# Sums of squares from ScalarE's accumulator in place of VectorE's reduction, in a fused decoder block

## The reference

```python
def rmsnorm(x, w, eps=1e-5):
    out = x * jax.lax.rsqrt(jnp.mean(x * x, axis=-1, keepdims=True) + eps)
    return out * w
q = rmsnorm((x @ Wq).reshape(B, T, H, D), q_rms_w)
k = rmsnorm((x @ Wk).reshape(B, T, H, D), k_rms_w)
scores = jnp.einsum('bthd,bshd->bhts', q, k) / sqrt(D) + bias   # causal
attn = softmax(scores)
y = rmsnorm(jnp.einsum('bhts,bshd->bhtd', attn, v), subln_w)
attn_out = y.transpose(0, 2, 1, 3).reshape(B, T, H * D) @ Wproj
```

## Time and profile before

| | |
|---|---|
| time, median of 3 runs | 435.72 us (434.96 to 436.02) |
| span of the profiled execution, first to last instruction | 432.9 us |
| TensorE busy | 401.9 us, 93% |
| its weight loads | 361.1 us, 83% |
| VectorE busy | 327.7 us, 76% |
| ScalarE busy | 254.4 us, 59% |
| GpSimd busy | 220.2 us, 51% |
| mean granted TensorE clock | 0.979 of full speed |
| chain that ended last, by engine | TensorE 86%, VectorE 5%, ScalarE 4% |

### The profile page before, as it was taken

One profiled execution on the slowest core, in us unless ns is written; L12 is line 12 of the kernel. 1 busy time (PEld: TensorE's weight loads), 2 busy tenths in 40 slices (PEclk: granted clock), 3 DMA queues, 4 the chain that ended last, 5 costly groups with the idle time before them and its releaser, 6 DMA issues.

```text
span 432.9 us, 9595 instructions
## 1 busy us (share of the span) xinstructions
PE 401.9 (93%) x2605; PEld 361.1 (83%) x2612; DVE 327.7 (76%) x1000; ACT 254.4 (59%) x750; POOL 220.2 (51%) x368
## 2 busy tenths in 40 slices
PE   4979999999999999999999999999999899999552
PEld 3668899999999999999999999999988677777321
DVE  0777987887797798788779779878822788888862
ACT  3486777677676776767767677676722333333321
POOL 3633667676675776767767677675501122222210
PEclk9999999999999999999999999999999999999965
DMA  8980010110101101011010110000000000000000
GB/s 223 316 251 2 2 36 3 38 37 0 36 0 36 36 0 36 0 36 36 0 36 0 36 36 0 0 0 0 0 2 0 2 0 15 12 14 12 13 14 24
DMA packets 21747, 14.52 MB, mean 34 GB/s; under 512 B 1760, under 2 KB 21472, under 8 KB 21728
## 3 DMA queue, kind: packets, MB, share of 16 engines
q1 hardware_dynamic: 21728, 14.29, 11.2%
HBM read 13.24 MB, written 1.05 MB: 33 GB/s over the span
## 4 chain that ended last, share of the span: by engine, by line
PE 86%; DVE 5%; ACT 4%; issue 2%; DMA 1%; POOL 1%; SPq 0%; POOLq 0%; DVEq 0%
PE ps L482 30%; PE ps L422 11%; PE ps L493 7%; PE ps L506 6%; PE ps L499 5%; PE ps L512 4%; PE ps L505 3%; PE ps L514 3%; PE ps L513 3%; PE ps L521 3%; PE ps L587 3%; PE ps L572 2%; ACT hT L696 2%; DMA x_sb<-in_x 1%; PE ps L557 1%
## 5 line engine op out<-in xcount | busy, mean ns | idle before, releaser
L315 POOL TENSOR_TENSOR qk_rstd<-qk_sum,minus_half 128x2 f32<-128x2 f32 x128 | 88.5, 692 | 92.6 <-DVE qk_sum L797 90.8
L482 PE MATMUL ps<-w_hi,xT_hi 128*128 128x384 f32 x256 | 96.9, 378 | 2.3 <-DVE qk_n L791 1.4
L482 PE MATMUL ps<-w_hi,xT_lo 128*128 128x384 f32 x256 | 86.5, 338 | 0.0
L482 PE MATMUL ps<-w_lo,xT_hi 128*128 128x384 f32 x256 | 86.3, 337 | 0.0
L797 DVE TENSOR_REDUCE qk_sum<-sq 128x2 f32<-128x258 f32 x128 | 53.6, 419 | 30.8 <-ACT sq L635 29.1
L635 ACT ACTIVATE sq<-ps 128x256 f32<-128x256 f32 x128 | 49.1, 384 | 34.6 <-PE ps L482 34.4
L791 DVE TENSOR_TENSOR qk_n<-ps,qk_rstd 128x256 f32<-128x256 f32 x128 | 54.2, 423 | 18.8 <-POOL qk_rstd L315 17.8
L422 PE MATMUL ps<-wp,yT 128*128 128x256 f32 x256 | 62.2, 382 | 0.0
L310 POOL TENSOR_TENSOR y_rstd<-y_sum,minus_half 128x2 f32<-128x2 f32 x64 | 49.0, 766 | 24.6 <-DVE y_sum L804 20.9
L673 ACT ACTIVATE sqy<-ps 128x258 f32<-128x258 f32 x64 | 24.8, 387 | 58.5 <-PE ps L514 58.5
L422 PEld LDWEIGHTS ps<-wp,yT 128*128 128x128 f32 x256 | 46.7, 190 | 5.9
(11 more groups left out here) (126 smaller groups left out, 846.9 us busy)
## 6 DMA issues: line engine op xcount, KB each, us to landing
w_raw<-in_L_attn_Wq SPq DMA_DIRECT2D x16, 128.0 KB, 2.2
w_raw<-in_L_attn_Wk SPq DMA_DIRECT2D x16, 128.0 KB, 2.3
w_raw<-in_L_attn_Wv SPq DMA_DIRECT2D x16, 128.0 KB, 2.3
wp<-in_L_attn_Wproj SPq DMA_DIRECT2D x1, 2048.0 KB, 16.1
ff_raw<-in_L_ffn_w_gate SPq DMA_DIRECT2D x1, 1024.0 KB, 8.6
ff_raw<-in_L_ffn_w_up SPq DMA_DIRECT2D x1, 1024.0 KB, 11.0
ff_raw<-in_L_ffn_w_down SPq DMA_DIRECT2D x1, 1024.0 KB, 13.0
out<-fin SPq DMA_DIRECT2D x8, 128.0 KB, 1.7
```

The source lines that it names most:

```text
L315: pool.tensor_tensor(qk_rstd[:, t, :], qk_sum[:, t, :], minus_half[:], ALU.pow).then_inc(s_rs[t], 1)
L482: last = pe.matmul(ps[:, t, 0:3 * D], xa[:, k, tok], wa[:, r, k * 3 * D:(k + 1) * 3 * D], start=(i == 0), stop=(i == len(parts) - 1))
```

## The change

ScalarE's Square is given an accumulator output, so it returns the sum along the columns beside the squares. Each accumulator output is one column of sums, so a square over q and k together, or over both tiles of y, is written as two instructions. VectorE's TENSOR_REDUCE instructions go. For q and k a VectorE addition puts 128 * eps on the two sums and writes qk_eps, which GpSimd reads; y's extra column stays, and GpSimd reads y_sum as ScalarE leaves it. The column of sq that held 128 * eps and its setting go. The semaphores change with it: the squares of tile t wait for the epsilon add of the step before (before: for its sum), and sqy waits for GpSimd's root of the y before (before: for VectorE's sum of it).

```diff
-        sq = sb("sq", [P, TT, 2, D + 1])
+        sq = sb("sq", [P, TT, 2, D])
         sqy = sb("sqy", [P, TT, VW])
+        qk_eps = sb("qk_eps", [P, TT, 2])
...
-            pool.memset(sq[:, :, :, D:D + 1], D * EPS).then_inc(s_const, 1)
...
-                        pool.wait_ge(s_ss[t], n + 1)
+                        pool.wait_ge(s_se[t], n + 1)
                         wait(pool, s_qkn[t], n)
-                        pool.tensor_tensor(qk_rstd[:, t, :], qk_sum[:, t, :], minus_half[:], ALU.pow).then_inc(s_rs[t], 1)
+                        pool.tensor_tensor(qk_rstd[:, t, :], qk_eps[:, t, :], minus_half[:], ALU.pow).then_inc(s_rs[t], 1)
...
                 def squares(t):
                     act.wait_ge(s_qkv[t], n + 1)
-                    wait(act, s_ss[t], n)
-                    act.activation(sq[:, t, :, 0:D], ps[:, t, 0:2 * D].rearrange("p (a d) -> p a d", a=2),
-                                   ACT.Square).then_inc(s_sq[t], 1)
+                    wait(act, s_se[t], n)
+                    for a in range(2):
+                        last = act.activation(sq[:, t, a], ps[:, t, a * D:(a + 1) * D], ACT.Square,
+                                              accum_out=qk_sum[:, t, a:a + 1])
+                    last.then_inc(s_ss[t], 1)
...
                     act.wait_ge(s_y, n - 1)
-                    wait(act, s_ssy, n - 2)
-                    act.activation(sqy[:], ps_y, ACT.Square).then_inc(s_sqy, 1)
+                    wait(act, s_ry, n - 2)
+                    for t in range(TT):
+                        last = act.activation(sqy[:, t], ps_y[:, t], ACT.Square, accum_out=y_sum[:, t:t + 1])
+                    last.then_inc(s_ssy, 1)
...
-                def sums(t):
-                    dve.wait_ge(s_sq[t], n + 1)
+                def add_eps(t):
+                    dve.wait_ge(s_ss[t], n + 1)
                     wait(dve, s_rs[t], n)
-                    dve.tensor_reduce(qk_sum[:, t, :], sq[:, t], AX.X, ALU.add).then_inc(s_ss[t], 1)
+                    dve.tensor_scalar(qk_eps[:, t, :], qk_sum[:, t, :], D * EPS, None, ALU.add).then_inc(s_se[t], 1)
...
-                if live(3):
-                    dve.wait_ge(s_sqy, n - 2)
-                    wait(dve, s_ry, n - 3)
-                    dve.tensor_reduce(y_sum[:], sqy[:], AX.X, ALU.add).then_inc(s_ssy, 1)
...
-                    sums(0)
+                    add_eps(0)
...
-                    sums(1)
+                    add_eps(1)
```

More of the change, by code:

```diff
@@ L176, in decoder_kernel @@
         s_v = [sem("v_tile0_copied"), sem("v_tile1_copied")]
-        s_sq = [sem("squares_tile0_done"), sem("squares_tile1_done")]
         s_ss = [sem("sums_tile0_done"), sem("sums_tile1_done")]
+        s_se = [sem("eps_tile0_added"), sem("eps_tile1_added")]
         s_rs = [sem("rstd_tile0_done"), sem("rstd_tile1_done")]
@@ L181, in decoder_kernel @@
         s_qkn = [sem("qk_tile0_normed"), sem("qk_tile1_normed")]
-        s_tqk, s_qkT, s_s, s_sc, s_p, s_tp, s_pT, s_y, s_sqy, s_ssy, s_yn, s_ty, s_yT = (sem(n) for n in (
+        s_tqk, s_qkT, s_s, s_sc, s_p, s_tp, s_pT, s_y, s_ssy, s_yn, s_ty, s_yT = (sem(n) for n in (
             "qk_turned", "qkT_copied", "scores_done", "scores_biased", "probs_done", "probs_turned",
-            "pT_copied", "y_done", "y_squared", "y_summed", "y_normed", "y_turned", "yT_copied"))
+            "pT_copied", "y_done", "y_summed", "y_normed", "y_turned", "yT_copied"))
         s_mv = [sem(f"mean_var{i}_done") for i in range(3)]
@@ L367, in _ @@
         def _(pe):
-            pe.wait_ge(s_const, 8)
+            pe.wait_ge(s_const, 7)
             def turn_x(b):
```

## The result

The changed kernel takes 449.42 us (median of 4 runs, 449.00 to 449.72) against 435.34 us for the kernel before on the same chip: a ratio of 1.0317 with an interval of 1.0296 to 1.0338, or 14.1 us slower. The profiled span went from 432.9 to 447.4 us, at the same granted clock (0.98).

A forecast was written before the change was run, and what follows sets the result against it. TensorE sets the pace, in a loop with ScalarE's chain from y to kT with little slack. Plain 9.5, feed-forward 4.6 and third feed-forward steps 2.8 add 16.9 to span 432.9, plus 2.8: 452.6 us, own range 446 to 459.

The forecast's parts named there:

- The loop's growth: Loop of y, ScalarE's chain, kT, scores, y: 0.48 us more chain, less slack, adds 16.9 us over 61 steps.
- Price of a square: On ScalarE, each replaced square was to take 0.50 instead of 0.26 us, 0.24 more.
- rivals 3 and 4: ScalarE readouts don't overlap, 481.9 us, in whole or part 0.13; accumulator needs no instruction, 432 to 436 us, 0.03.
- The two constants of the loop: TensorE's part: kT's end to weight load 0.05 us, load to next sqy 1.63, read in an early step.
- Two squares count, the third is free: sqy and tile 0's square lie in the loop and add 0.48 us; tile 1's, after kT, costs nothing.
- Rival 1: Added ScalarE work is covered and VectorE's relief counts: faster, 431.6 us; chance 0.07.
- Rival 2: prob waits for VectorE's scores anyway, hiding sqy's growth: one square counts, 2.3 us, 438.0 us; chance 0.11.
- VectorE and GpSimd at nothing: Sums removed from VectorE, adds and roots cost zero; at most 4.1 us of pT waits could come back.
- Plain steps: Steps without feed-forward copy, 4.43 us: loop 4.20 becomes 4.68, growth 0.25, 38 steps, 9.5 us.
- first two feed-forward steps: Steps with a feed-forward copy, 4.65 us: loop 4.46 becomes 4.94, growth 0.29, 16 steps, 4.6 us.
- The third feed-forward step: Third such step of eight, with the loop's branch, 4.69 us: loop becomes 5.09, growth 0.40, 7 steps, 2.8 us.
- the difference of span and median: Median of the runs lies 2.8 us above the profiled span; left as it is, 449.8 becomes 452.6 us.

The follow-up runs named there:

- the four kernels above: Accumulator for some squares only, others as before: tile 1 431.81 us, y 436.62, tile 0 437.56, tile 0 and y 450.64.
- the runs with one square: Accumulator for one square ahead of kT, the others as in the kernel before: y 436.62 us, tile 0 437.56 us.
- tile 1 alone: Accumulator only for the square of tile 1 of q and k, tile 0 and y summed on VectorE as before: 431.81 us, once more 432.75.
- tile 0 alone: Accumulator only for the square of tile 0 of q and k, the others as in the kernel before: 437.56 us, ratio 1.0062.
- copies added: Kernel before with three more ScalarE copies of 128 columns a step: ahead of tile 0's v 453.41 us, ahead of tile 1's v 435.75.
- v moved: Copy of v of tile 0 put behind kT: in the kernel before 434.26 us, with tile 1's accumulator 431.86, in the changed kernel 439.90.
- y alone: Accumulator only for the square of y, the others as in the kernel before: 436.62 us, ratio 1.0045.
- tile 0 and y: Accumulator for the squares of tile 0 and y, tile 1 summed on VectorE as before: 450.64 us, ratio 1.0358.
- yT or v moved, or both: Changed kernel with yT copied by VectorE 435.70 us, with v of tile 0 copied behind kT 439.90, with both 435.69.
- copies in the chain: Kernel before with three more ScalarE copies of 128 columns a step ahead of tile 0's v: 453.41 us, ratio 1.0411.

## Why the prediction was right, point by point

The forecast was 452.6 us and the time is 449.42, inside its own range; the mechanism is the one that it named. The loop's growth, the main term, was 16.9 us in the forecast; from sqy of step 2 to sqy of step 63, the same 61 steps, the trace has 15.4.

**Price of a square.** Taken: 0.16 for a half, 0.09 for a readout, 0.50 for two pairs. Measured: 221.84 to 222.00 is 0.16, 222.00 to 222.09 is 0.09, and two pairs hold ScalarE for 0.50 to 0.52. The chain from sqy's start to kT's end went from 2.52 to 3.00 us: 0.48, as worked out. So the single readout in the preparation, with 256 columns around it, was a good trial for readouts with 128 (rivals 3 and 4 fall). The groups of instructions by line and shape (count, busy us, mean ns of one, idle before) give the lengths:

```profile
L801 DVE TENSOR_SCALAR qk_eps<-qk_sum 128x2 f32<-128x2 f32 x128 | 21.6, 169 | 90.8 <-ACT sq L636 87.3
...
L636 ACT ACTIVATION_READ_ACCUMULATOR sq<-ps 128x1 f32 x256 | 53.4, 209 | 0.0
...
L676 ACT ACTIVATION_READ_ACCUMULATOR sqy<-ps 128x1 f32 x128 | 25.4, 199 | 0.0
```

The new addition was priced from one on 128x3 (170 ns) and takes 169. The 78.8 us of readouts are the trap of this view: their lengths overlap what follows, and the queue pays 384 x 0.09 = 35 us for them.

**The two constants of the loop.** 0.05 and 1.63 us, read in an early step, came back to the hundredth in the middle of the stage (224.57 to 224.62, 224.62 to 226.25).

**Two squares count, the third is free.** Shown by the four kernels above. Rival 1 (covered by the less loaded engine) fails: ScalarE had 0.78 us of idle time ahead of sqy in a plain step and 0.59 ahead of tile 1's square, both outside the chain. The prediction's reading, that ScalarE's idle time lies ahead of sqy, left out the second place (29.6 us in all); since it lies behind kT, the forecast didn't suffer. Rival 2 (the scores hide sqy's growth) fails: ScalarE's list of waits has no row for VectorE, and in the plain step above prob starts 0.09 us after the last readout of sqy. Only its number fits elsewhere, since it is what the slack leaves of one square alone: 2.3 us, where the runs with one square gave 1.7 and 2.6.

**VectorE and GpSimd at nothing.** Right in the loop; ahead of the first kT the way got 0.5 us shorter, which goes with VectorE's shorter work there. The relief of VectorE is worth something, 3.1 us with tile 1 alone, close to the 4.1 us of the wait for pT, but in the changed kernel it lies under the wait for kT.

**The sum: two terms were too large.** Plain steps of the loop grew by 0.25 as taken (4.43 to 4.68), the first two feed-forward steps of a trip by 0.29 (4.66 to 4.95). The third feed-forward step was to grow by 0.40 and grew by 0.26: 4.69 (204.13 to 208.82) became 4.95. This is ScalarE in the changed kernel at that step:

```profile
211.95 0.28 ACT L676 ACTIVATE sqy<-ps 128x129 f32<-128x129 f32 x1 [0.89 <-PE ps L514]
...
212.47 0.37 ACT L686 COPY wdT<-ps 128x256 bf16 x1
212.73 0.42 ACT L646 ACTIVATE prob<-score,neg_max 128x128 f32<-128x128 f32 x1
...
214.80 0.42 ACT L664 COPY kT<-ps 128x256 f32<-128x256 f32 x1
...
216.90 0.28 ACT L676 ACTIVATE sqy<-ps 128x129 f32<-128x129 f32 x1 [0.82 <-PE ps L514]
```

Before, the copy of wdT in the same place was followed later by prob:

```profile
204.42 0.37 ACT L682 COPY wdT<-ps 128x256 bf16 x1
204.83 0.40 ACT L644 ACTIVATE prob<-score,neg_max 128x128 f32<-128x128 f32 x1
```

From the copy to prob it was 0.41 us and is 0.26. Between these two instructions lies the branch of the loop, and the prediction had taken its 0.15 us as a fixed part of the chain. In the changed kernel it has gone. Six of the seven steps of this kind end with a jump back to the loop's start, so this is 6 x 0.14 = 0.8 of the 3.2 us by which the forecast was too high. The second term is the early steps. The forecast gave each of steps 2 to 4 the growth of a plain step, 0.75 us in all, and together they grew by nothing (-0.07). Three steps at the loop's edges (7, 61 and 62) grew by 0.42 each, 0.3 more than taken, which makes up the difference to the 15.4 us. The rest lies in the start, 1.3 us earlier, and in the difference of span and median (2.8 us in the forecast, 2.0 after); about 0.4 us, outside the counted steps, went the other way.

The gap itself, from the start of the wdT copy to that of prob, goes with two things. It is 0.41 to 0.43 us only in the six steps that jump back; the same two instructions are 0.25 apart where the loop is entered and where it is left. And it is that long only in the eight kernels where the square of y is one instruction (the one before, and those built on it with tile 1 alone, tile 0 alone, copies added or v moved). In the six where that square is split in two (the changed one, y alone, tile 0 and y, and the changed one with yT or v moved, or both) it is 0.25 in these steps too. It also makes the difference between the two runs with one square: with tile 0 alone, which keeps the gap, the third step of a trip grew by 0.16 us, with y alone, which loses it, by 0.01; six times this is the 0.9 us between 1.7 and 2.6. The kernel with copies in the chain kept the gap too, with a third step of 5.10 us (215.96 to 221.06 between two starts of sqy):

```profile
215.96 0.39 ACT L676 ACTIVATE sqy<-ps 128x258 f32<-128x258 f32 x1 [1.22 <-PE ps L514]
221.06 0.39 ACT L676 ACTIVATE sqy<-ps 128x258 f32<-128x258 f32 x1 [1.24 <-PE ps L514]
```

The 5.09 of the forecast was thus right for a chain with the gap. A likely reason is that the queue gets through its branch while the longer run of instructions ahead is still under way; that is argued and not shown.

## What to carry to other kernels

Before work is moved to the engine with the most idle time, find where that idle time lies: an engine that is woken by the bottleneck, runs a chain without a gap and releases the bottleneck again is on the critical loop however low its share is. Measure the loop (start of the chain to its end, plus the consumer's way back) against the step; the difference is the slack. Here, what was added ahead of the release cost little up to the slack (0.45% and 0.62%) and was paid in full, in every step, beyond it, while the same work behind the release went into idle time and cost nothing that could be told from the noise. Then split the change by place: one third of this one, alone, was a gain of 0.5% to 0.6%, and the whole a loss of 3.2%.

## What the runs showed of the hardware

The branch gap above is one such thing. Another is that two of VectorE's three quantising instructions of a feed-forward step changed their lengths though nothing in them changed. By groups of instructions in the changed kernel (x24 is three a trip and three more):

```profile
L783 DVE TENSOR_SCALAR ff_round<-ff_round 128x256 f32<-128x256 f32 x24 | 15.8, 657 | 0.8
L781 DVE TENSOR_SCALAR ff_round<-ff_raw,w_inv 128x256 f32 x21 | 7.2, 345 | 0.0
```

and in the kernel before:

```profile
L777 DVE TENSOR_SCALAR ff_round<-ff_raw,w_inv 128x256 f32 x21 | 12.6, 601 | 0.0
L779 DVE TENSOR_SCALAR ff_round<-ff_round 128x256 f32<-128x256 f32 x24 | 7.1, 295 | 0.8
```

The first of the three (L777, now L781) fell from 601 to 345 ns, the second (L779, now L783) rose from 295 to 657. The sum of y no longer stands ahead of them, so they start earlier against GpSimd's split of the weights (L280); in every kernel that keeps that sum the first starts 0.24 us or more into the split. The timeline of the changed kernel:

```profile
207.33 0.34 DVE L781 TENSOR_SCALAR ff_round<-ff_raw,w_inv 128x256 f32 x1
207.40 0.87 POOL L280 TENSOR_TENSOR w_lo<-w_raw,w_hi 128x256 fp32r<-128x256 f32 x1
207.71 0.71 DVE L783 TENSOR_SCALAR ff_round<-ff_round 128x256 f32<-128x256 f32 x1
```

The first starts 0.07 us ahead of the split, runs beside it for 0.27 and stays short; the second starts 0.31 into it and is long. In the kernel before, the split lay at 200.44 to 201.17, and the first started 0.24 into it (200.68, 0.64 long). So it isn't enough to lie beside the split: the one of these two that starts while it is under way takes about twice as long, all 21 times that they meet in either kernel, and the one that starts just ahead of it doesn't, but then the split takes 0.87 instead of 0.73 us. What this cost here no run isolates, but a duration read in one place may not hold in another.

The Trainium skill, "SBUF — State Buffer", section "Who interferes with whom", states that VectorE shares a pair of ports with GpSimd, which a tensor_scalar in a two-port mode takes as a whole, so that the later of the two is blocked. The trace agrees in that the later one is the long one on either side, VectorE's second with 657 against 295 ns, and the split, when VectorE's first has the start, with 0.87 against 0.73 us; that either stood blocked for the difference, and in which mode the tensor_scalar ran, no row shows.
